# A graph network's sorted messages stored as three bfloat16 parts in records of 100 words

## What is computed

```python
h = jnp.maximum(_layernorm(x, axis=-1), 0.0)
transformed = node_features @ kernel                      # 12500 x 64
messages = edge_vals[:, None] * transformed[edge_col]     # one row of 64 per edge
aggregated = jax.ops.segment_sum(messages, edge_row, num_segments=N_NODES)
return jax.nn.relu(aggregated + bias)
...
x = x + _L0_gnn_ref(h, src, dst, edge_weight, L0_gnn_kernel, L0_gnn_bias)
```

## Time and profile before

| | us |
|---|---|
| median of 3 runs | 17359.45 (17355.03 to 17366.96) |
| span of the profiled execution, first to last instruction | 17336.1 |
| ordering loop, first to last scatter issued | 366.1 to 2486.0 |
| block sums, loop | 2552 to about 3078 |
| zeroing, first to last DMA issued | 63.9 to 331.1 |

### The profile page before, as it was taken

How to read it: one execution, slowest core, us unless ns; L and a number is a source line. 1 busy time by engine, 2 the same in 40 slices (tenths; PEclk the granted TensorE clock), 3 DMA queues, 4 the chain that set the end, 5 groups by cost and what they waited for, 6 DMA issues and landing times. The chain is left out here.

```text
span 17336.1 us, 347951 instructions
## 1 busy us (share of the span) xinstructions
PE 12043.3 (69%) x77017; PEld 8987.5 (52%) x77018; DVE 12515.5 (72%) x30887; ACT 7365.4 (42%) x19165; POOL 11501.3 (66%) x11855
## 2 busy tenths in 40 slices
PE   4443338599997577777777767777787888844444
PEld 2222225466665466665666656666545555533333
DVE  7777769777776788887888878888765666634443
ACT  1111129555554566665666656666441222200000
POOL 2777750377775577775777757777407777767777
PEclk7555555677776555665555565555696777755555
DMA  6333344333335222222222232222495666511111
GB/s 234 96 94 94 93 94 123 108 102 103 102 102 90 73 58 58 58 58 70 58 58 58 58 76 58 58 58 58 149 389 128 182 180 181 174 51 26 26 26 32
DMA packets 1329349, 1689.67 MB, mean 97 GB/s; under 512 B 835210, under 2 KB 903562, under 8 KB 1296591
## 3 DMA queue, kind: packets, MB, share of 16 engines
q1 hardware_dynamic: 899089, 875.57, 17.3%
q0 software_dynamic: 412640, 597.16, 15.7%
q10 hardware_dynamic: 17474, 215.22, 3.2%
HBM read 1072.24 MB, written 618.81 MB: 98 GB/s over the span
## 5 line engine op out<-in xcount | busy, mean ns | idle before, releaser
L2166 POOL DMA_INDIRECT gat_from_src<-gat_src_dram,gat_src_at x4992 | 4815.2, 965 | 1709.8 <-issue 1520.2
L3157 PE MATMUL rel_ps_sum<-all_node,rel_msg 128*64 128x128 f32 x6656 | 1418.8, 384 | 1487.3 <-DVEq L3116 1456.8
L2971 POOL DMA_INDIRECT rel_from_src<-typed_dram,rel_src_at x1664 | 1644.2, 988 | 1087.1 <-ACT rel_src_at L2986 607.3
L2387 PE MATMUL gat_ps_sum<-all_node,gat_msg 128*80 128x128 f32 x9984 | 2268.3, 420 | 41.7 <-DVE gat_msg L2281 7.5
L3157 PEld LDWEIGHTS rel_ps_sum<-all_node,rel_msg 128*64 128x64 f32 x6656 | 1138.0, 199 | 1963.5 <-DVEq L3116 1206.5
L1630 POOL DMA_INDIRECT all_node<-hyp_dst_dram,hyp_src_at x1768 | 1725.9, 976 | 604.4 <-issue 508.0
L2387 PEld LDWEIGHTS gat_ps_sum<-all_node,gat_msg 128*80 128x80 f32 x9984 | 2057.9, 252 | 102.0 <-issue 41.7
L1094 POOL DMA_INDIRECT bucket_dram<-all_node,order_index x1664 | 1613.6, 970 | 524.8 <-issue 506.9
L2971 POOL DMA_INDIRECT rel_from_src<-typed_next_dram,rel_src_at x1664 | 1589.9, 955 | 559.1 <-issue 492.7
L2329 DVE TENSOR_TENSOR gat_sums_sums<-gat_sums_sums,gat_ps_sum 80x128 f32 x4992 | 1393.5, 279 | 382.5 <-DVE gat_sums_sums L2329 212.5
L2291 DVE TENSOR_TENSOR_SCAN gat_ps_log<-gat_masks,gat_top,gat_ps_log 8x1024 f32<-8x1024 bf16 x624 | 1461.9, 2343 | 229.4 <-DVE gat_sums_sums L2329 220.8
(11 more groups left out here) (571 smaller groups left out, 26975.5 us busy)
## 6 DMA issues: line engine op xcount, KB each, us to landing
typed_dram<-typed_res SPq DMA_DIRECT2D x98, 2080.0 KB, 7.4
typed_next_dram<-rel_res ACTq DMA_DIRECT2D x98, 2080.0 KB
gat_relrow<-in_rows_dram SPq DMA_DIRECT2D x624, 256.0 KB
all_node<-gcn_table_dram SPq DMA_DIRECT2D x1664, 48.0 KB
gat_from_src<-gat_src_dram,gat_src_at POOLq DMA_INDIRECT x4992
bucket_dram<-by_dst_zero POOLq DMA_DIRECT2D x48, 1326.0 KB, 6.6
gsum_rec<-bucket_dram SPq DMA_DIRECT2D x221, 288.0 KB, 2.8
all_node<-lo_rows_dram SPq DMA_DIRECT2D x221, 256.0 KB
```

Of the source, the lines that this page charges most:

```text
L2166: nc.gpsimd.indirect_dma_start(from_src[:, q, k, :], None, g.gat_src[:, :], bass.IndirectOffsetOnAxis(ap=src_at[:, q, k:k + 1], axis=0)).t ...
L2387: last = nc.tensor.matmul(ps_sum[0:rows, k, :], msg[:, q % 2, k, :], member[:, q, k, :], start=True, stop=True)
L2971: nc.gpsimd.indirect_dma_start(from_src[:, q, k, :], None, table[:, :], bass.IndirectOffsetOnAxis(ap=src_at[:, q, k:k + 1], axis=0)).then_ ...
L3157: last = nc.tensor.matmul(ps_sum[0:D, k, :], msg[:, q % 2, k, :], member[:, q, k, :], start=True, stop=True)
```

## The change

A record grows from 72 to 100 words: three parts of 64 bfloat16 numbers (96 words, `PARTS_W`), three index fields, one word spare. The ordering loop makes the parts. ACT now writes the weighted message as float32 into scratch memory (`scale`, lead 1), and copies the first part and the second part from its upper halves into the record (`fill`, lead 0). DVE makes the rest between (`rest_of`) and the third part (`third_of`), both with lead 0. The scratch is the tile `g.zero`, so DVE and ACT wait at the start of the stage until all zeroing DMAs are through, as POOL did before. POOL waits for `third` too. `look` on PE waits for `scaled` in place of `filled`. In the block sums `first_rest` and `third_part` are gone, PE reads the parts from the record, and DVE makes five of the one-hot matrices, ACT three (`KA` from 5 to 3). The zeroing has 68 DMAs of 2600 words a partition in place of 48 of 2652; they are dealt out as 13, 6, 19 and 30.

```diff
-RW = 72
+RW = 100
+PARTS_W = 3 * D // 2
-KA = 5
-CLEARS = 48
+KA = 3
+CLEARS = 68
...
-                clear_buckets(nc, g, pool, 0, 8)
+                clear_buckets(nc, g, pool, 0, 13)
...
-                clear_buckets(nc, g, pool, 8, 13)
+                clear_buckets(nc, g, pool, 13, 19)
...
-                clear_buckets(nc, g, pool, 22, CLEARS)
+                clear_buckets(nc, g, pool, 38, CLEARS)
...
+        whole, rest = (g.zero[:, n * 2 * K * D:(n + 1) * 2 * K * D].rearrange("p (s k d) -> p s k d", s=2, k=K)
+                       for n in range(2))
+
+        def part(q, n):
+            return rec[:, q].bitcast(BF16)[:, :, n * D:(n + 1) * D]
+
+        def upper(ap):
+            return ap.bitcast(BF16)[:, :, 1::2]
...
                     pool.wait_ge(filled, ready(c))
+                    pool.wait_ge(third, ready(c))
                     pool.wait_ge(placed, ready(c))
...
+                for s in range(2):
+                    act.wait_ge(g.zeroed[s], 16 * (CLEARS // 2))
...
-                def fill(c, q, i):
+                def scale(c, q, i):
                     act.wait_ge(weighed, ready(c))
                     act.wait_ge(looked, ready(c))
+                    act.wait_ge(third, free2(c))
                     for k in range(K):
-                        last = nc.scalar.activation(rec[:, q, k, 0:D], ps_dst[q % 2][:, k, :], ACT.Copy,
+                        last = nc.scalar.activation(whole[:, q % 2, k, :], ps_dst[q % 2][:, k, :], ACT.Copy,
                                                     scale=weight[:, q, k:k + 1])
-                    last.then_inc(filled, 1)
-                rounds(act, [(fields, 1), (fill, 0)])
+                    last.then_inc(scaled, 1)
+
+                def fill(c, q, i):
+                    act.wait_ge(scaled, ready(c))
+                    nc.scalar.activation(part(q, 0), upper(whole[:, q % 2]), ACT.Copy)
+                    act.wait_ge(rest_made, ready(c))
+                    nc.scalar.activation(part(q, 1), upper(rest[:, q % 2]), ACT.Copy).then_inc(filled, 1)
+                rounds(act, [(fields, 1), (scale, 1), (fill, 0)])
...
+                for s in range(2):
+                    dve.wait_ge(g.zeroed[s], 16 * (CLEARS // 2))
                 v.memset(rec[:, :, :, :], 0.0).then_inc(cleared, 1)
...
+                def rest_of(c, q, i):
+                    dve.wait_ge(scaled, ready(c))
+                    dve.wait_ge(filled, free2(c))
+                    v.tensor_tensor(rest[:, q % 2], whole[:, q % 2], upper(whole[:, q % 2]), ALU.subtract
+                                    ).then_inc(rest_made, 1)
+
+                def third_of(c, q, i):
+
+                    dve.wait_ge(rest_made, ready(c))
+                    v.tensor_tensor(part(q, 2), rest[:, q % 2], upper(rest[:, q % 2]), ALU.subtract
+                                    ).then_inc(third, 1)
+
...
-                             (turned_ones, 2), (tile_b, 1), (add(2), 1), (tile_c, 1), (add(3), 1), (eight_a, 1),
+                             (rest_of, 0), (tile_b, 1), (turned_ones, 2), (third_of, 0), (add(2), 1), (tile_c, 1),
+                             (add(3), 1), (eight_a, 1),
...
-                    pe.wait_ge(filled, free2(c))
+                    pe.wait_ge(scaled, free2(c))
...
-                def first_rest(c, q, i):
+                def ones(c, q, i):
                     dve.wait_ge(rec_in[q], 16 * (i + 1))
                     dve.wait_ge(summed, free2(c))
-                    v.tensor_tensor(rest[:, q % 2], rec[:, q, :, 0:D], upper(rec[:, q, :, 0:D]), ALU.subtract
-                                    ).then_inc(rest0, 1)
...
-                rounds(dve, [(first_rest, 1), (ones, 1), (third_part, 1), (add, 0)], BCHUNKS)
+                rounds(dve, [(ones, 1), (add, 0)], BCHUNKS)
...
-                    pe.wait_ge(part2, ready(c))
                     pe.wait_ge(members, ready(c))
...
-                        clears=(13, 22))
+                        clears=(19, 38))
```

More of the change, by code:

```diff
@@ L1039, in edges_ordered @@
             "step_c step_p opened cleared halved kept mark_a")
+        scaled, rest_made, third = ph.sems("scaled rest_made third")
         rel_in, win, landed = ([ph.sem(f"{n}{q}") for q in range(4)] for n in ("rel_in", "win", "landed"))
@@ L1128, in _ @@
                 v = nc.vector
-                for q in (turned, members, count_c, split, placed):
+                for q in (turned, members, count_c, split, placed, rest_made, third):
                     dve.sem_inc(q, START)
+                for s in range(2):
+                    dve.wait_ge(g.zeroed[s], 16 * (CLEARS // 2))
                 v.memset(rec[:, :, :, :], 0.0).then_inc(cleared, 1)
@@ L1337, in _ @@
                 v = nc.vector
-                for q in (members, rest0, part2, added):
+                for q in (members, added):
                     dve.sem_inc(q, START)
@@ L1386, in product @@
                         at = window[:, ds(regs[k], 1), :].rearrange("p o d -> p (o d)")
-                        for n, own in enumerate((upper_of(rec[:, q, k, 0:D]), upper_of(rest[:, q % 2, k, :]),
-                                                 last_part[:, q % 2, k, :])):
-                            last = nc.tensor.matmul(at, member[:, q % 2, k, :], own, start=False, stop=k == K - 1 and n == 2)
+                        for n in range(3):
+                            last = nc.tensor.matmul(at, member[:, q % 2, k, :], part(q, k, n), start=False,
+                                                    stop=k == K - 1 and n == 2)
                     last.then_inc(summed, 1)
```

26 lines of the change are left out of this document (9 added, 17 removed).

## The result

The changed kernel takes 17487.5 us (median of 4 runs, 17469.6 to 17492.4) beside 17359.8 for the kernel before on the same chip: a ratio of 1.0073, 95% interval 1.0061 to 1.0084. On a second chip it was 1.0083 (1.0067 to 1.0098). I had forecast 17374 and no difference that can be measured.

| | before | after | difference | forecast |
|---|---|---|---|---|
| start to first scatter of the ordering loop | 366.1 | 403.1 | +37.0 | +25.5 |
| first to last scatter | 2119.9 | 2213.6 | +93.8 | 0 |
| last scatter to first record read | 59.6 | 60.7 | +1.2 | 0 |
| block sums, to the last addition | 531.1 | 509.8 | -21.3 | -11 |
| the rest | 14259.5 | 14280.4 | +20.9 | 0 |

A forecast was written before the change was run, and what follows sets the result against it. POOL's scatters were taken to bound the ordering loop, DVE the block sums. Terms +16 + 0 + 3 + 6.5 + 0 - 11 = +14.5 gave a span of 17350.6 and, with 23.35 kept for the median, 17374; range 17340 to 17430.

The forecast's parts named there:

- What bounds the two stages: Ordering loop: POOL issues scatters without a break, 10.20 us a turn; block sums: DVE's own length, 2.42 us.
- DVE's turn, 10.05 against POOL's 10.20: Ordering loop: two added operations lengthen DVE's turn from 8.83 to 10.05 us; POOL stays the bound, so 0.
- Rival A: Ordering loop: DVE takes over as the bound; at a turn of 10.4 us +42, total 17416; chance 0.26.
- The step that failed: Ordering loop: gathers beside subtractions are only 8 ns dearer, so new subtractions cost scatters at most +13 us, taken as 0.
- Zeroing beside the projection, +16: Projection: more zeroing on full DMA engines costs +16 us, bounds +6 to +20.
- `bucket_places` and start of the ordering loop, +3 and +6.5: DVE waits for the last zeroing and a larger memset, +3 us; first scatter waits for the third part, +6.5.
- Block sums, -11: Block sums: PE is late next, its turn 2.34 us after 2.39, so -11 us, bounds 0 and -25.
- Rival B: Block sums: PE's gap shrinks (17285) or its clock rises (17244); chance 0.12.
- The rest, 0: Stages outside the ordering loop, block sums and what precedes them: no change forecast, 0.

The follow-up runs named there:

- PSUM kernel: Changed kernel with each ordering-loop subtraction on DVE reading one input from PSUM, third part made two steps later: ratio 1.0015, loop 2118.3 us.
- reordered run: Changed kernel with the same instructions in another order on DVE in the ordering loop: ratio 1.0107, loop 2257.9 us.
- idle subtraction from PSUM: Kernel before plus one unused DVE subtraction of 512 elements a turn in the ordering loop, one input in PSUM: ratio 1.0014, loop 2122.4 us.

## Why the prediction was wrong, point by point

- **What bounds the two stages**: right. POOL without a break in the ordering loop, and its waits behind it.
- **DVE's turn, 10.05 against POOL's 10.20**: right. DVE still waits after the change, and in the PSUM kernel the loop runs at its old 2118 us with the same number of operations. Rival A did not happen. DVE's own length came out below the 10.05: some 9.8 us, an estimate from the turn of 10.64 (2213.6 / 208) less the waits of 0.63 and 0.19.
- **The step that failed**: "*The gathers beside such subtractions, only 8 ns dearer, speak against it*", on what a subtraction of DVE does to a scatter. I took the 8 ns between two means, 978 and 970, for its price: +13 us at most, and 0 in the sum. The timeline of the kernel before, hyperbolic layer, shows what the mean hid (L1807 and L1820 are DVE operations with two SBUF inputs):

```profile
3411.05 0.96 POOL L1630 DMA_INDIRECT all_node<-hyp_dst_dram,hyp_src_at  x1 [0.30 <-issue]
...
3412.24 0.69 DVE L1807 TENSOR_TENSOR hyp_part<-hyp_from_h,hyp_small 128x512 f32<-128x512 f32 x1
...
3412.32 1.44 POOL L1630 DMA_INDIRECT all_node<-hyp_dst_dram,hyp_src_at  x1 [0.30 <-ACT hyp_from_h L1665]
...
3413.95 0.68 DVE L1820 TENSOR_TENSOR hyp_last_part<-hyp_rest 128x512 bf16<-128x512 f32 x1
3414.06 1.39 POOL L1630 DMA_INDIRECT all_node<-hyp_dst_dram,hyp_src_at  x1 [0.30 <-issue]
```

  A gather takes 0.95 there, and the two that start beside such an operation 1.44 and 1.39: 0.83 and 0.82 after it ends. The same relation stood in the trace before the change. Of the 624 gathers between 3300 and 4100 us 58 take more than 1.02 us, 55 of them beside one of the three two-input operations. So 978 is 0.95 with some gathers of 1.0 to 1.4 in it, and the base of another kind of transfer is no measure for this one. What the runs showed in its place: about one scatter a turn held up, 93.8 us in the loop, where the sum had 0. The Trainium skill (SBUF — State Buffer, "SBUF: two separate sides") states the rule that I set aside: two SBUF inputs take a port that a GpSimd operation reading SBUF needs, and the loser blocks until the end. The runs here agree as to two inputs in SBUF and one in PSUM (2213 against 2118 us). The other half of that rule in the Trainium skill, that an operation in a fast mode which takes both ports blocks as well, fits `turned_ones` (1024 elements in 0.48 us) where it ran already at a scatter's start and in the reordered run, though not the four cases of the kernel before and the eight of the changed one.
- **Zeroing beside the projection, +16**: the stage behind it started its zeroing at 265.4 in place of 248.2, +17. Right.
- **`bucket_places` and start of the ordering loop, +3 and +6.5**: DVE began the ordering loop at 375.9 in place of 347.0, 29 us later; 17 are the projection's, which leaves 12, where I had 2.4 ahead of this point. The stage ends about 10 us after POOL's last zeroing (364.9 to 374.9), where I had counted the landing of two (6.6); and the gaps between the 30 averaged 3.43 us, not 3.31. From there to the first scatter were 27.3 us in place of 19.1, +8 where I had 7.3 with the larger memset.
- **Block sums, -11**: -21. The mechanism was right (PE is late next, and its gap is its registers), the gain twice what I had. I put a gap of 0.52 from a turn of the kernel before into every turn; in the changed kernel two turns of four are 2.13 to 2.19 (zeros 0.40 to 0.46 after the start of the last product), one is 2.24 to 2.29 and the one at the back edge 2.60 to 2.64. The mean is 2.30 in steady state against 2.34. Rival B did not happen: the granted clock stayed 0.50.
- **The rest, 0**: +21 in the profiled execution, and the medians of the second chip (+152) leave some 41 beyond the first four rows. Open, see below.

## What to carry to other kernels

Where the GpSimd queue issues indirect DMAs back to back, a VectorE operation beside it costs by where its inputs lie and when it starts, not only by its length: read one input from PSUM, or expect a scatter like these that starts beside it to end 0.85 us after it. That covers operations with two inputs; a long one-input operation such as `turned_ones` can hold a scatter up too. To cost such an effect, look at the timeline for the longest instances of an instruction and what ran beside them; a mean over hundreds with a base of its own hides one in eight. A plain transfer that shares a queue with scatters is worth trying on another queue: with 30 zeroings moved to SyncE the first scatter came 9.5 us earlier, with 40 it came 20 us earlier.

## What else the runs showed

- A scatter of 128 records costs POOL the same for 72 and 100 words: 970 and 969 ns.
- `turned_ones` lengthens scatters of the kernel before as well, by little. Where it runs already when a scatter starts, the scatter ends 0.83 to 0.92 us after it (3 scatters there, 11 in the PSUM kernel, 38 with the idle subtraction from PSUM). Where it begins 0.35 to 0.53 us into a scatter, the scatter can end 0.11 to 0.20 us after it, at 1.03 to 1.16: that is 35 of the 40 scatters above 1.02. So a scatter seems to need the shared thing a second time; this was read from the traces and not tried.
- One scatter can be kept waiting for 90.6 us by 190 VectorE operations in a row (558 ns each, both inputs in SBUF, no idle time). With the same operations and scatters only, most scatters got through in 1.13 us.
- The time that PE spends on its registers: 8 of them 0.7 us from the last product to the next, 32 of them over 2 us.
- Open: the later layers. The part behind the block sums took 14243.8 us (from the next DVE operation on) in the kernel before and 14241.3 with the larger record and its zeroing alone, but 14247 to 14307 in all the others, among them the one with an idle subtraction from PSUM (14263.4) and the one whose only change is the zeroing's queue (14271.1), neither of which touches a later stage. In the fourth layer the 1664 gathers of the first half average 988 and 986 ns in the first two and 994 to 1013 in the others. Whether the phase between VectorE and GpSimd, which matters in the ordering loop, is what shifts there was not tried.
